# Gated two-layer block on one core: in the last stage, rows of two of three blocks are turned by VectorE and two transfers

## The reference, cut to what matters

```python
def _L1_ffn_ref(x, U, V, W1, b1, W2, b2):      # x: layer-normalised rows
    h = jax.nn.relu(jnp.einsum('bsd,de->bse', x, W1) + b1)
    alpha = jax.nn.softmax(jnp.einsum('bse,ek->bsk', h, W2) + b2, axis=-1)
    vx = jnp.einsum('krd,bsd->bskr', V, x)
    uvx = jnp.einsum('kdr,bskr->bskd', U, vx)
    return jnp.einsum('bsk,bskd->bsd', alpha, uvx)
...
x = x + jnp.tanh(g_ffn[1]) * _L1_ffn_ref(_layernorm(x, axis=-1), ...)
```

## Time and profile before

| | us |
|---|---|
| median of 3 runs | 1345.37 (1344.8 to 1349.57) |
| the profiled execution | 1344.79 |
| its span, first to last instruction | 1343.0 |

### The profile page before, as it was taken

The page is one execution under the profiler, slowest core; times in us unless marked ns, Lnnn a source line. Parts: engine busy times, 40 slices in busy tenths (PEclk is TensorE's granted clock), DMA queues, the critical chain, the costliest instruction groups (busy, mean ns, idle before and its releaser), DMA issues.

```text
span 1343.0 us, 20310 instructions
## 1 busy us (share of the span) xinstructions
PE 1321.1 (98%) x7404; PEld 1069.2 (80%) x7404; DVE 932.6 (69%) x1805; ACT 517.6 (39%) x1569; POOL 404.2 (30%) x461
## 2 busy tenths in 40 slices
PE   7999999999999999999999999999998899999998
PEld 6888888888887788778887888788876687778877
DVE  5765676675775868775778667776888787846533
ACT  3544445454564331231123111411127777732210
POOL 4212323231256252101120111113426866630000
PEclk9999999999999999999999999999999999999999
DMA  8755454444572232210221012112324556555431
GB/s 298 230 169 160 147 168 142 157 149 134 186 224 74 83 87 71 83 40 16 64 83 53 18 40 89 42 48 67 104 92 145 182 181 205 173 197 156 149 110 55
DMA packets 131655, 163.51 MB, mean 122 GB/s; under 512 B 15436, under 2 KB 85196, under 8 KB 131556
## 3 DMA queue, kind: packets, MB, share of 16 engines
q1 hardware_dynamic: 131556, 162.22, 38.0%
HBM read 109.74 MB, written 52.43 MB: 121 GB/s over the span
## 4 chain that ended last, share of the span: by engine, by line
PE 91%; DVE 4%; ACT 3%; DMA 1%; issue 0%; POOL 0%; SPq 0%; DVEq 0%; ACTq 0%; POOLq 0%
PE bank L118 89%; PE bank L121 2%; ACT P L124 2%; DVE st L152 1%; DVE STG L130 0%; DVE sm L146 0%; DVE AH L130 0%; DVE AR L130 0%; DMA XR<-in_x_dram 0%; ACT AR L124 0%; ACT STG L124 0%; DMA STG<-in_WqT_dram 0%; ACT bank L124 0%; DVE AH L127 0%; DVE PTV L127 0%
## 5 line engine op out<-in xcount | busy, mean ns | idle before, releaser
L118 PE MATMUL bank<-XT,AR 128*128 128x512 f32 x1152 | 280.1, 393 | 0.1
L118 PE MATMUL bank<-AR 128*128 128x512 f32 x1056 | 258.5, 395 | 1.7 <-DVE AR L130 1.7
L118 PEld LDWEIGHTS bank<-XT,AR 128*128 128x128 f32 x1152 | 213.9, 188 | 48.2 <-issue 1.5
L124 ACT ACTIVATE STG<-bank,b1c 128x512 f32<-128x512 f32 x128 | 88.3, 690 | 387.1 <-PE bank L118 313.7
L118 PEld LDWEIGHTS bank<-AR 128*128 128x128 f32 x1056 | 194.2, 188 | 47.8 <-issue 2.8
L118 PE MATMUL bank<-AR,CT 128*128 128x512 f32 x768 | 191.3, 392 | 0.0
L118 PE MATMUL bank<-AR,AH 128*128 128x512 f32 x768 | 185.9, 390 | 0.0
L127 DVE CAST AH<-STG 128x512 fp32r<-128x512 f32 x192 | 91.1, 475 | 112.6 <-PE bank L118 98.7
L118 PEld LDWEIGHTS bank<-AR,AH 128*128 128x128 f32 x768 | 143.6, 188 | 30.6 <-issue 1.1
L118 PEld LDWEIGHTS bank<-AR,CT 128*128 128x128 f32 x768 | 140.2, 188 | 27.0 <-issue 0.4
L127 POOL CAST BA<-STG 128x256 fp32r<-128x256 f32 x64 | 31.3, 489 | 396.1 <-PE bank L118 241.0
(11 more groups left out here) (143 smaller groups left out, 1818.9 us busy)
## 6 DMA issues: line engine op xcount, KB each, us to landing
XR<-scr SPq DMA_DIRECT2D x64, 256.0 KB, 3.0
pscr<-PYZ SPq DMA_DIRECT2D x30, 512.0 KB, 2.9
PYZ<-pscr SPq DMA_DIRECT2D x120, 128.0 KB, 2.9
XR<-in_x_dram SPq DMA_DIRECT2D x32, 256.0 KB, 4.1
XR<-lscr SPq DMA_DIRECT2D x128, 64.0 KB, 2.0
scr<-XR SPq DMA_DIRECT2D x32, 256.0 KB, 2.1
pscr<-STG SPq DMA_DIRECT2D x16, 512.0 KB, 2.6
PTV<-pscr SPq DMA_DIRECT2D x64, 128.0 KB, 2.8
```

Of the source, the lines that this page charges most:

```text
L118: return self.e.matmul(o, w, x, start=start, stop=stop, skip_group_check=True) if self.e else Nothing()
L124: return self.e.activation(o, x, func, **kw) if self.e else Nothing()
```

## The change

For the blocks 2 and 3 of the last stage (all but block 1 of the three that are turned there) the four turns on TensorE are gone. VectorE turns 32x32 blocks into the second half of `MSK`; SyncE stores each tile and brings it back in place; ScalarE and VectorE split it. The order of `split4` and `out4` on VectorE, the place of the row loads for block 3 (now between the stores of `vx`, as for block 2 before) and the place of the loads for the sums (now behind the `vx` transfers) change with it.

```diff
         def by_blocks(ph, m):
-            return (ph, m) in ((0, 1), (0, 2), (0, 3), (1, 0), (1, 1), (1, 2), (1, 3), (2, 0))
+            return (ph, m) in ((0, 1), (0, 2), (0, 3), (1, 0), (1, 1), (1, 2), (1, 3), (2, 0), (3, 2), (3, 3))
...
         def ly(ph, m):
+            if ph == 3:
+                return MSK[:, 1, :]
...
         def ly_free(ph, m):
+            if ph == 3:
+                return t_ly[3, 2, 3] if m == 3 else ps.full(("s3", 15, 3))
...
@@ TensorE
                     for tb in range(1, 4):
-                        if more:
-                            ln_turn(3, m + 1, tb - 1, ring8.next())
                         out4(m - 1, tb)
                         if tb == 1:
                             logits_b(m)
-                    if more:
-                        ln_turn(3, m + 1, 3, ring8.next())
...
@@ ScalarE
                 if m:
                     if more:
-                        ln_turn(3, m + 1, 0)
+                        ln_split(3, m + 1, 0)
                     split4(m - 1, 3)
...
-                    if more and (tb >= 1 or m == 0):
-                        ln_turn(3, m + 1, tb)
+                    if m == 0:
+                        ln_turn(3, 1, tb)
+                    elif more and tb >= 1:
+                        ln_split(3, m + 1, tb)
...
@@ VectorE
                     split4(m - 1, 0)
-                    split4(m - 1, 1)
                     if more:
                         for tb in range(4):
                             ln_pre(3, m + 1, tb)
-                        for tb in range(4):
+                        ln_norm(3, m + 1, 0)
+                        ln_blocks(3, m + 1, 0)
+                        for tb in range(1, 4):
                             ln_norm(3, m + 1, tb)
-                    out4(m - 1, 0)
+                    split4(m - 1, 1)
+                    if more:
+                        ln_blocks(3, m + 1, 1)
                     split4(m - 1, 2)
                     if more:
-                        ln_turn(3, m + 1, 0)
-                    out4(m - 1, 1)
+                        ln_blocks(3, m + 1, 2)
+                    out4(m - 1, 0)
+                    if more:
+                        ln_blocks(3, m + 1, 3)
                     split4(m - 1, 3)
                     a = logits(m)
+                    out4(m - 1, 1)
                     if more:
-                        ln_turn(3, m + 1, 1)
+                        ln_split(3, m + 1, 0)
                     out4(m - 1, 2)
                     if more:
-                        ln_turn(3, m + 1, 2)
+                        ln_split(3, m + 1, 1)
                     out4(m - 1, 3)
                     if more:
-                        ln_turn(3, m + 1, 3)
+                        ln_split(3, m + 1, 2)
...
+                    elif more and tb == 0:
+                        ln_split(3, m + 1, 3)
...
@@ SyncE
                 if m:
+                    if more:
+                        ln_store(3, m + 1, 0)
+                        ln_back(3, m + 1, 0)
                     for tb in range(4):
-                        n = 4 * ((m - 1) % 2) + tb
+                        if more and tb < 3:
+                            ln_store(3, m + 1, tb + 1)
+                            ln_back(3, m + 1, tb + 1)
                         x4_store(m - 1, tb)
-                        if more:
+                if more:
+                    for tb in range(4):
+                        v_store(m, tb)
+                        if m < 2 and tb:
+                            for k in ((0,), (1,), (2, 3))[tb - 1]:
+                                ln_load(3, m + 2, k)
+                        if tb:
+                            v_back(m, tb - 1)
+                    v_back(m, 3)
+                    if m:
+                        for tb in range(4):
+                            n = 4 * ((m - 1) % 2) + tb
                             e.wait_ge(*t_x4[n][m - 1])
                             e.wait_ge(*stored(3, m + 1, tb))
                             e.dma(X4[:, n, :], rows(3, m + 1, tb)).then_inc(*d_x4[n].mark(m + 1))
```

More of the change, by code:

```diff
@@ L2588, in sync @@
                             e.dma(X4[:, n, :], rows(3, m + 1, tb)).then_inc(*d_x4[n].mark(m + 1))
[L2589 to L2600, removed]
                 else:
```

## The result

The changed kernel takes 1354.83 us in the median against 1344.58 us before, measured again beside it: a ratio of 1.0069, 95% interval 1.0057 to 1.0081. It is slower: by 9.3 us by the ratio, 10.25 us by the two medians. 1352.2 us had been forecast, with a range from 1346.5 to 1356.5 us. The profiled execution took 1354.48 us, its span is 1352.7 us, and the mean granted clock fell from 1.000 to 0.995.

A forecast was written before the change was run, and what follows sets the result against it. TensorE, with matmuls at 98% of the span, was taken as the bound. From 1344.79 us, -3.4 for turns, +1.7 and +6.5 for waits, +2.0 for clock gave 1351.6, or 1352.2 us against the median; range 1346.5 to 1356.5 us.

The forecast's parts named there:

- What is removed: Last stage, TensorE: four turns cost 1.71 us in place, so two blocks give back 3.4 us.
- The path: VectorE's turns wait for SyncE's stores, the split stands behind tile 3's turn, TensorE's last output product needs it 21.1 us in.
- Block 1: Last stage: the split ends at 1241.5, due 1239.8, so TensorE stands for 1.7 us (bounds 0 and 3.5).
- Block 2: Last stage: first store lands in 4.7 us behind loads; TensorE stands for 6.5 us (bounds 3.8 and 8.5).
- The clock: TensorE's clock falls after the 5.8 us idle stretch in block 2, costing 2.0 us (bounds 0 and 4.7).
- the one at 1064.38: TensorE idle of 1.66 us before the last stage; three passes then took 0.96 us, read as no clock loss.
- the passes at the start of the run: After 7.31 us of idling, four passes took 3.02 us at 13.75 against 1.88 us at 23.57, taken as slow clock.
- A: Rival: the same stalls in blocks 1 and 2, but the clock stays up; 1350.2 us, chance 31%.
- B: Rival: the sum loads do not hold up block 2's first store, which lands in 2.0 us; 1347.5 us, chance 12%.
- C: Rival: the store chain hides under the products, no wait is left; 1342.0 us, a gain of 0.25%, chance 7%.
- the parts named for "slower": Chance of over 1352.1 us: half the likeliest case and a little beyond, a sixth of A, all longer stalls; together 0.40.

The follow-up runs named there:

- e8: Changed kernel with block 2's sum loads later, row transfers ahead of output stores, splits ahead of turns and late statistics: 1341.58 us, ratio 0.9973 to the kernel before.
- e2: Changed kernel with VectorE's splits ahead of turns that wait for a store, and in block 2 ScalarE's half of the last one: 1351.97 us.
- e3: Changed kernel with 8, 6 and 24 extra passes filling TensorE's idle stretches before three output products, no wait removed: 1352.35 us.
- e10: Changed kernel profiled once more, nothing changed; ratio not measured, stage 132.77 us.
- e7: Changed kernel with only block 2 turned the new way, block 3 left to TensorE's transposes, moved loads kept: 1346.52 us, ratio 1.0012 to the kernel before.
- e4: Changed kernel with block 2's sum loads later, row stores and returns ahead of output stores, two splits ahead of turns: 1343.85 us, ratio 0.9987 to the kernel before.

## Why the prediction came out as it did

*What is removed.* The 3.4 us were right. e8's stage is 124.28 - 120.90 = 3.4 us shorter with every wait gone.

*The path.* It was right in all its steps: VectorE's turns wait for the stores, the splits stand behind the turns, TensorE waits for the splits, in both blocks; `h4` of blocks 2 and 3 never waits in the changed kernel.

*Block 1.* 1.7 us forecast, 2.3 us measured. The chain's head was 0.3 us late against the block's start (store at 1229.07, 11.0 us after it; 10.7 us forecast), and the second train of four DMAs took 2.00 us to issue, not 1.75.

*Block 2.* 6.5 us forecast, 7.6 us measured. In this profile the landing of the first store behind the four loads took 5.7 us, not 4.7, outside the upper bound of 5.3 us that I had from the nearest row. The other 0.4 us (9.9 us forecast, 10.3 measured) came in between that landing and `out4(1, 3)`, and the store itself was issued 0.2 us earlier in its block than forecast. The 4.7 us was no bad size for all that: e2, e3 and e10 have 4.9, 4.7 and 4.8 us with the same DMAs ahead of the store. Why one landing took 1 us longer is not shown. The split of the waiting was less well seen: some 0.5 us and 5.8 us in one piece were forecast, and the trace has 1.37 us, a slow product, and 4.28 us.

*The clock.* 2.0 us forecast for the one long stretch, 3.9 us measured, of which 2.2 us behind the long stretch and 1.6 us behind the wait in block 1. I had given the short waits no price, on the strength of the one at 1064.38. That failed: half the granted clock stood behind waits of 1.99 and 1.37 us. In the second profile of the changed kernel (e10) it did not fail: the clock cost 2.1 us, all of it behind the long stretch. That the forecast is so near the cost of the long stretch is luck: 2.0 us was picked between bounds of 0 and 4.7 us, from no row of its own. Its argument rests on the passes at the start of the run, whose granted clock is recorded as 1.00; no run here shows that they were slow because of the clock. By the rule of the Trainium skill, page "TensorE: Matmul & The Clock Gate", section "The HAM clock gate", the array drops to 1.2 GHz on idling; the profile after agrees, with 0.50 granted in the stretches shown. Behind the 2.05 us of e10 the clock did not drop, so idling alone does not decide it.

*Rivals.* A (the clock stays up) fell with e3 and the windows. B (the loads do not hold up the store) fell with the landings of 4.7 to 5.7 us behind them, against 2.0 to 3.0 us without. C (the chain hides) is not what the change does, but it is what e8 does: the same turns, splits and transfers, in another order.

The total was 2.6 us short: 1.7 us of waits and 1.9 us of clock too little, less the 0.7 us by which the stages ahead were shorter and 0.2 to 0.3 us between profiled run and median. One sum of the forecast does not come out: the parts named for "slower" (about 0.25 for half of the likeliest case and a little beyond, 0.05 for a sixth of A, 0.05 for the longer stalls) make 0.35, not 0.40.

## What to carry to other kernels

A turn taken from the engine that bounds the kernel pays its full time only if every wait that it brings is kept off the in-order queues that feed this engine: put the instructions that the bounding engine is waiting for ahead of those that wait for a transfer. Count a store that is waited for with what stands in the DMA queue ahead of it: with four 256 KB loads there that no one is in a hurry for, it landed in 4.7 to 5.7 us, without them in 2.0 to 3.0 us. An idle stretch of TensorE can cost 1.6 to 2.3 us more than its length. Here the same removed work gave 9.3 us of loss in one order and 3.6 us of gain in another.

## What was not expected of the hardware

What was not expected is the clock behind short waits. The changed kernel was profiled a second time:

> The changed kernel profiled once more, nothing changed, for the clock: waits of TensorE of 2, 1.4 and 4.3 us had half the granted clock behind them in its first profile, while e7's wait of 2.4 us had none. Theory (a short idle stretch may or may not cost the clock, a long one does): behind the long wait the granted clock is 0.50 again, behind the one in block 1 it may be either. Rival (the idle's length alone decides): both as in the first profile.

As the theory had it, in this profile block 1's wait of 2.05 us has no slow clock behind it, where the first profile's 1.99 us at the same place had one. Nor have the waits of 0.23 and 0.78 us in block 2 a slow clock behind them; only the one of 5.93 us has. TensorE's timeline of e10:

```profile
1242.86 13.92 PE L118 MATMUL bank<-AR 128*128 128x512 f32 x60 [2.05 <-DVE AR L130]
...
1285.12 5.15 PE L118 MATMUL bank<-AR 128*128 128x512 f32 x12 [5.93 <-DVE AR L130]
```

Over all the profiles of this stage, half the clock stands behind waits of 1.37, 1.85, 1.99, 2.11, 3.89, 4.28, 4.74 and 5.93 us, and the full clock behind 0.23, 0.38, 0.39, 0.60, 0.78, 1.58, 1.71, 2.05 and 2.38 us. What decides between 1.4 and 2.4 us stays open; the length of the wait alone does not. The products behind such a wait lost 1.6 to 2.3 us each time that the clock fell. A single profile of a kernel with such waits can therefore be some microseconds off the median, as that of e4 was.

The record of the granted clock says 1.00 over the first 17 us of the kernel before too, where four passes took 3.02 us. Whether the clock or something else made them slow, no run here shows; in the last stage the record agrees with the lengths of the passes.
